# Attention with relative positions: a unit's loads and its store of heads issued in one place on the queue

## The reference, cut to what matters

```python
x = x + 0.5 * ffn(layernorm(x))           # x: (8, 1024, 256)
x = x + attn(layernorm(x))
x = x + 0.5 * ffn(layernorm(x))

# attn: B = 8, S = 1024, H = 16 heads of dh = 16
q, k, v = xn @ Wq + bq, xn @ Wk + bk, xn @ Wv + bv      # each (B, S, H, dh)
p       = (sinusoidal_pe(S, 256) @ Wp)                  # (S, H, dh)
content = einsum('bihd,bjhd->bhij', q + u_bias, k)
pos     = relative_shift(einsum('bihd,jhd->bhij', q + v_bias, p))
attn    = softmax((content + pos) * dh ** -0.5)
out     = einsum('bhij,bjhd->bihd', attn, v).reshape(B, S, 256) @ Wo + bo
```

## Time and profile before

| | us |
|---|---|
| median of 3 runs | 3573.16 (3572.06 to 3573.51) |
| the profiled execution, its own time | 3570.63 |
| its span in the profile | 3568.8 |
| TensorE busy | 3338.3 (94%) |
| ScalarE busy | 2310.6 (65%) |
| VectorE busy | 1811.5 (51%) |
| packets of the SP queue, share of 16 DMA engines | 94.2% |

### The profile page before, as it was taken

The page is one execution under the profiler, slowest core; times in us unless marked ns, Lnnn a source line. Parts: engine busy times, 40 slices in busy tenths (PEclk is TensorE's granted clock), DMA queues, the critical chain, the costliest instruction groups (busy, mean ns, idle before and its releaser), DMA issues. The chain is left out here.

```text
span 3568.8 us, 85700 instructions
## 1 busy us (share of the span) xinstructions
PE 3338.3 (94%) x24380; PEld 1826.7 (51%) x24380; DVE 1811.5 (51%) x3599; ACT 2310.6 (65%) x3253; POOL 1241.6 (35%) x1212
## 2 busy tenths in 40 slices
PE   7996999999999999999999999999999999999988
PEld 5673444444444444444444444444444444444467
DVE  6871444444444444444444444444444444444457
ACT  2443676676776667666666667776767676776633
POOL 1111333333333333333333333333333333333310
PEclk9997999999999999999999999999999999999989
DMA  4655999999999999999999999999999999999962
GB/s 147 204 186 196 372 377 371 376 373 373 374 377 374 376 374 374 372 375 372 375 373 371 372 370 376 372 375 375 377 374 371 377 372 372 377 376 375 339 184 100
DMA packets 439308, 1221.81 MB, mean 342 GB/s; under 512 B 59360, under 2 KB 143840, under 8 KB 439264
## 3 DMA queue, kind: packets, MB, share of 16 engines
q1 hardware_dynamic: 435824, 1219.72, 94.2%
q10 hardware_dynamic: 3440, 1.53, 0.2%
HBM read 624.38 MB, written 596.65 MB: 342 GB/s over the span
## 5 line engine op out<-in xcount | busy, mean ns | idle before, releaser
L776 DVE CUSTOM_DVE_ANT_0 at_pos_in<-at_ps_con,at_pos_in 128x1024 f32<-128x1024 f32 x1024 | 1254.1, 1225 | 1583.4 <-PE at_ps_con L664 1353.8
L813 POOL TENSOR_SCALAR at_pos_in<-at_pos_in,at_neg_max 128x1024 f32<-128x1024 f32 x1024 | 1145.5, 1119 | 1906.9 <-DVE at_neg_max L776 1906.9
L744 ACT ACTIVATE at_pos_out<-at_ps_pos 128x1024 f32<-128x1024 f32 x1024 | 1048.9, 1024 | 602.5 <-PE at_ps_pos L664 602.5
L753 ACT ACTIVATE at_prob<-at_ps_turn 128x512 f32<-128x512 f32 x2048 | 1110.7, 596 | 362.6 <-PE at_ps_turn L687 362.6
L664 PE MATMUL at_ps_con<-at_right,at_left 32*128 32x512 f32 x4096 | 1156.2, 640 | 149.3 <-DVE at_neg_max L776 147.3
L687 PEld LDWEIGHTS at_ps_turn<-keep_ident,at_pos_in 128*128 128x128 f32 x8192 | 898.7, 143 | 628.7 <-issue 426.8
L664 PE MATMUL at_ps_pos<-at_right,at_left 32*128 32x512 f32 x4096 | 1163.7, 644 | 25.8 <-DMA at_right<-scratch_pos_rows 17.9
L687 PE MATMUL at_ps_turn<-keep_ident,at_pos_in 128*128 128x128 f32 x8192 | 1113.7, 279 | 2.3
L699 PE MATMUL at_ps_pv<-at_prob,at_v_aug 128*32 128x512 f32 x4096 | 545.3, 605 | 0.8 <-issue 0.8
L664 PEld LDWEIGHTS at_ps_con<-at_right,at_left 32*128 32x128 f32 x4096 | 308.2, 183 | 341.2 <-ACT at_pos_out L744 196.7
L710 PEld LDWEIGHTS at_ps_head<-keep_fold,at_head_T 128*128 128x128 f32 x2048 | 247.8, 191 | 195.7 <-DVE at_head_T L784 148.6
(11 more groups left out here) (85 smaller groups left out, 1227.6 us busy)
## 6 DMA issues: line engine op xcount, KB each, us to landing
scratch_scores<-at_pos_out SPq DMA_DIRECT2D x1024, 512.0 KB, 7.7
at_pos_in<-scratch_scores SPq DMA_DIRECT2D x1024, 512.0 KB, 7.8
at_left<-scratch_qk_rows SPq DMA_DIRECT2D x512, 64.0 KB, 5.2
scratch_qk_rows<-fr_qk SPq DMA_DIRECT2D x48, 512.0 KB, 5.8
fr_x<-in_L_attn_x_dram SPq DMA_DIRECT2D x16, 512.0 KB, 6.1
scratch_x<-fr_x_bo SPq DMA_DIRECT2D x16, 512.0 KB, 3.2
scratch_values<-fr_values SPq DMA_DIRECT2D x8, 1024.0 KB, 5.2
at_right<-scratch_pos_rows SPq DMA_DIRECT2D x256, 32.0 KB, 5.9
```

The costliest lines, as they stand in the source:

```text
L744: act.activation(pos_out[:, t.slot, :], ps_pos[:, :, :].rearrange("p a m -> p (a m)"), ACT.Copy)\
L753: act.activation(prob[t.t // QUAD % 2][:, 4 * n:4 * n + 4, k * P:(k + 1) * P], ps_turn[:, n, :].rearrange("p (j i) -> p j i", i=P), ACT.Exp)\
L776: dve.tensor_tensor_reduce(pos_in[:, t.slot, :], ps_con[:, :, :].rearrange("p a m -> p (a m)"), pos_in[:, t.slot, :], -SCALE, 3.0e38, ALU. ...
L813: pool.tensor_scalar(pos_in[:, t.slot, :], pos_in[:, t.slot, :], -1.0, neg_max[:, t.slot:t.slot + 1], ALU.mult, ALU.add).then_inc(shifted, 1)
```

## The change

`load_qv`, `load_qk` and `store_head` are all issued in the first step of a unit, after `write` and `read_back` of that step. The guard of `load_qv` (a unit of positional scores done) and those of `load_qk` (content scores and values done) are the same expressions, taken at the same unit. `store_head` is issued in the first step of the unit that comes two after its own, which is three steps later than before, and the unrolled end is longer for this reason: 17 steps past the last two units in place of 8. The added steps hold nothing but the last stores.

```diff
             with eng.Fori(1, last) as r:
                 for t in range(BODY):
                     step(r, t)
-            for t in range(BODY + 8):
+            for t in range(BODY + 17):
                 step(last, t)
...
             def step(r, t):
                 w = Tile(r, t + LEAD)
                 if w.real():
-                    if w.i == 0 and Tile(r, t + LEAD + TILES).real():
-                        load_qv(Tile(r, t + LEAD + TILES))
                     write(w)
                 back = Tile(r, t + LEAD - READ_LAG)
                 if back.real():
                     read_back(back)
-                if t % TILES == 1 and Tile(r, t - 1 + TILES).real():
-                    load_qk(Tile(r, t - 1 + TILES))
-                done = Tile(r, t - TILES)
-                if t % TILES == 5 and done.real():
-                    store_head(done)
+                if t % TILES == 0:
+                    if Tile(r, t + LEAD + TILES).real():
+                        load_qv(Tile(r, t + LEAD + TILES))
+                    if Tile(r, t + TILES).real():
+                        load_qk(Tile(r, t + TILES))
+                    done = Tile(r, t - 2 * TILES)
+                    if done.real():
+                        store_head(done)
```

## The result

The changed kernel takes 3847.76 us (median of 4 runs, 3833.05 to 3854.11) against 3573.34 in the same comparison: a ratio of 1.0762, 95% interval 1.0727 to 1.0796, so 274 us or 7.6% slower. The forecast was slower too, but 3690, and the time lies above the range's 3795.

A forecast was written before the change was run, and what follows sets the result against it. It took TensorE, 94% busy, as the bound, with DMA engines nearly full too. A late read's 1.13 us less the present 0.20, times 126 units, added 117 us to 3570.6; with 2.5 us to the median, 3690, range 3600 to 3795.

The forecast's parts named there:

- the place and the length of the burst: Ten small DMAs in a row in a unit's first step: begin at 4.04 us, take some 7.7 us to issue.
- the sum: Tile 5's read leaves at 12.56 us, lands at 17.56, costing 1.13 us in a unit, net 0.93.
- the prediction's estimate of 3.5 us with the write ahead: Faster rival, chance 0.09: by the skill's rule tile 5's read lands within the 3.87 us allowed, giving 3547 us.
- the term "s": TensorE's loss from tile 5's late read: its landing time less 16.43 us, 1.13 us in a unit.
- the present 0.20 us: Kernel before: late reads cost some 0.20 us in a unit; the change was to remove this.
- TensorE's path sets the unit and the queue refills for nothing: After tile 5, reads keep up, 2.8 us against a 3.09 us step, and the queue fills again by unit's end.
- The rival "the DMA engines become the bound": During the ten small DMAs the full DMA engines idle, lengthening each unit by 1.2 to 2.0 us; chance 0.20.
- its sign (several reads late in a row): Profile sign that the DMA engines are the bound: several reads in a row are late and not one.
- the length of the queue at the burst as given, 8.9 us: A read takes 8.9 us to land before small DMAs; each takes about 0.37 away, leaving 5.2 after ten.
- each theory by itself: Two theories: TensorE loses by the late read behind the ten DMAs, or DMA engines run dry and the unit grows.
- A's wait: VectorE's wait for the late read behind the ten small DMAs, on which the whole forecast rested.
- the second case: DMA engines become the bound, 3720 to 3820 us; 2.0 us a unit gives 252 us, 3823 at most; chance 0.20.

The follow-up runs named there:

- after_unread: Changed kernel with VectorE adding fixed zeros and waiting for no read-back, all DMAs and SyncE's waits kept: 3828.63 us, ratio 1.0642 to the kernel before.
- deep_reads: Changed kernel with reads taking input x, so SyncE waits for no write to land, VectorE still waiting for each read: 3867.11 us, ratio 1.0758.
- free_reads: Changed kernel with VectorE waiting for no read and reads taking input x, so SyncE waits for no write to land: 3566.83 us, ratio 0.9983.
- thin_loads: Changed kernel with the eight loads of left and right carrying a quarter of their columns, same count of DMAs: 3897.57 us, ratio 1.0829.
- the spread kernel: Kernel before with the same ten small DMAs spread over the unit's first six steps, one or two behind each read: 3565.79 us, ratio 0.9937.
- balanced: Kernel before with load_qk moved from a unit's second step to its fifth, store of heads from sixth to seventh: 3680.19 us, ratio 1.0287.

## Why the prediction was wrong

**Right: the place and the length of the burst.** In the unit shown, the ten leave from 1538.64 to 1546.52, 7.9 us (forecast 7.7), and the read behind them lands after 4.7 us (forecast 5.0, with 4.3 and 6.0 as ends). It leaves 1547.38 - 1533.95 = 13.43 us into the unit, though, 0.87 later than the 12.56 of the sum, most of it from a burst that begins at 4.69 and not at 4.04.
The Trainium skill's formula ("DMA: Bandwidth & Descriptors", Anatomy of one DMA) gives the prediction's estimate of 3.5 us with the write ahead, which is too low here. Content scores of tile 6 follow those of tile 5 after 1553.76 - 1549.30 = 4.46 us in place of 3.09, so this one read costs 1.37 where the sum had 1.13, with TensorE already 0.5 us late when it came.

**Wrong: the term "s", as a size.** The sum priced one late read and said of the next that it keeps up, and of the present 0.20 us that it goes away. The second read landed so late that tile 7's scores came 3.45 us after tile 6's (0.36 more), the third was late again, and nothing was given back. 108 late reads in 39 units stand against the one in a unit of the forecast. Of the 2.65 us of this unit, tile 5's read is 1.37, close to its term; what lies around it makes the larger part of the miss.

**Wrong: the step beneath it, that TensorE's path sets the unit and the queue refills for nothing.** The sum let a late read cost TensorE time and treated the DMA engines as able to catch up, with "the queue fills again by the end of the unit". It does fill again (9.3 us at the burst), but not for nothing: SyncE, which had 9.6 us of landing waits in 1000, has 92.5. `after_unread` shows the size: without the late read's wait, the loss is still 6.4%. How much of a burst the DMA engines themselves could make up, with their share at 1.02 and single microseconds at 400 to 420 GB/s, isn't shown, since TensorE sets the pace in the runs whose queue stays long. The rival "the DMA engines become the bound" was nearer, with its sign (several reads late in a row) come true, but it took 1.2 to 2.0 us a unit for idle engines alone. In the unit shown, idleness around the burst is 1.1 us, and no term had the wait for landings.

**Left out: what keeps the queue short.** The forecast took the length of the queue at the burst as given, 8.9 us. Two loops bound it. SyncE may issue the read of tile t + 4 only when the write of tile t + 5 has landed, three writes back. And the writes wait for copies that wait, through TensorE's one buffer of content scores and VectorE, for the reads to land. Either loop alone holds the time at 1.06 to 1.08 (`after_unread` has the first, `deep_reads` the second); with both gone (`free_reads`) the queue is 12 us long and a burst of 7.9 us is covered. That is why each theory by itself failed: A's wait is real and sufficient, but not necessary.

Two slips of the prediction's arithmetic change nothing: the second case's 252 us give 3825 us and not 3823, and traffic in proportion to 3690 us would be 360 GB/s and not 358.

**What stays open.** Why the engines move only 164 and 242 GB/s at a share of 0.9 in two of the three microseconds behind the restart was seen and not explained. What moving `load_qk` alone costs wasn't run. `thin_loads` was expected to equal the changed kernel and was not faster; whether it is slower can't be said, since the two ran on different chips.

## What to carry to other kernels

When DMA engines run at a share near 1, count a group of small DMAs by what SyncE needs to issue it (0.7 to 0.8 us each here) against the time that the queue ahead of it holds, and ask which waits bound that length: a read that must wait for an earlier write's landing, and a consumer that holds back the next write. The loss here grew faster than the group, with reads that took 8 to 9 us to land: against the spread kernel, groups of four and five (3.0 and 3.5 us of issue) cost 0.6%, nine in a row (7.1 us) 4.8%, ten (7.9 us) 8.3%. One or two small DMAs behind each large one were the cheapest order that was run, provided that what they load is due later than the queue is long (`balanced` shows the price if it isn't).

## What the runs showed of the hardware

Eight loads of 16 rows cost their issue and not their bytes: with 16 and 8 KB in place of 64 and 32 there was no gain (1.0829 against 1.0762). Packets under 2 KB keep the DMA engines busy and move little: 193 GB/s at a share of 1.09 in a microsecond of `free_reads` in which they were 144 of 185. Behind a gap, in the unit shown, the engines were busy to 0.89 and 0.93 and moved 164 and 242 GB/s, against 406 ahead of it. With a queue of 12 us, reads and writes of 512 KB ran at 375 GB/s, with one of 8 us at 372; TensorE sets the pace in both, so neither is shown to be the most that the engines can do. DMAs of one queue don't land in the order of their issue: the load issued at 1541.93 landed after 4.2 us, at 1546.1, ahead of the read issued at 1537.49 that landed at 1546.8.
